# Cross-attention scored three tiles ahead, and a convolution in rounds of two blocks, in a twelve-sublayer kernel

## The chip, the cores and the metric

The kernel runs on one core of a Trainium2 chip. The metric is the device time of one execution in microseconds, as the median of several runs. The engines are PE (matrix products, with its weight loads PEld), DVE (vector), ACT (activation functions), POOL, and SP, which here only issues transfers.

## What is computed

A model of four layers with three sublayers each works on 2 x 1024 tokens of width 256 in float32. Each sublayer is added to its input and the sum normalised. The change touches two of the twelve:

```python
def _L2_xattn_ref(query, key, value, Wq, bq, Wk, bk, Wv, bv, Wo, bo):
    Q = jnp.einsum('bsd,de->bse', query, Wq) + bq
    K = jnp.einsum('bsd,de->bse', key, Wk) + bk
    V = jnp.einsum('bsd,de->bse', value, Wv) + bv
    scale = 1.0 / jnp.sqrt(jnp.asarray(D, Q.dtype))
    scores = jnp.einsum('bqd,bkd->bqk', Q, K) * scale
    attn = jax.nn.softmax(scores, axis=-1)
    out = jnp.einsum('bqk,bkd->bqd', attn, V)
    return jnp.einsum('bsd,de->bse', out, Wo) + bo
...
def _L3_attn_ref(x, W_in, conv_w, conv_b, W_out):
    h = jnp.einsum('bld,df->blf', x, W_in)
    a, g = jnp.split(h, 2, axis=-1)
    h = a * jax.nn.sigmoid(g)
    hc = jnp.transpose(h, (0, 2, 1))
    y = lax.conv_general_dilated(hc, conv_w, window_strides=(1,), padding=[(K - 1, 0)], ...) + conv_b[None, :, None]
    y = jax.nn.silu(y)
    y = jnp.transpose(y, (0, 2, 1))
    return jnp.einsum('blf,fd->bld', y, W_out)
```

The attention has one head of width 256 and 154 keys. The convolution is causal, with 4 taps, and each of its 512 channels has its own weights.

## The kernel before

Activations are held feature-major (`XT`, 128 partitions x 2 chunks x 2048 tokens) and token-major (`Xtok`, 16 tiles of 128 tokens). Each sublayer is a row of phases. A `phase` opens a block in which every engine runs its own list in the order of the code, with waits on counting semaphores; a barrier of all engines ends it. Nothing of a phase overlaps the next one. There are eight PSUM banks of 128 x 512 floats, `K.bank`. On an engine an instruction that reads what the one before it wrote has a `drain` or a semaphore wait ahead of it.

**Attention, `L2_xattn` (from L895).** After the projections one phase (L913) goes through `NT` = 16 tiles of 128 tokens. For each tile PE scores it (`score`, L924: 128 x 154), DVE takes the row maximum and scales it (`maximum`, L957 and L959), ACT takes the exponential with the row sum as a second result (L984), DVE takes the reciprocal of the sum and multiplies (L971, L973), PE transposes the result in two pieces (L945, L946), and ACT copies these into `PT` (L997, L998). For each block of four tiles PE multiplies with the values (`values`, L934), both halves of the features in a row, and DVE copies the result out (`output`, L964). PE scores tile t+1 ahead of the transposes of tile t. Scores have two banks (0, 1), as `probs` has two buffers, transposes two banks (2, 3) and value products four (4 to 7). After a block's fourth tile its values come behind the next tile's transposes.

**Convolution, `L3_attn` (from L1060).** One phase (L1074) goes through 16 blocks of 128 channels x 512 tokens. For each PE computes a and g (L1089; block n uses the pair of banks n % 4), ACT takes the sigmoid of g (L1100), DVE multiplies it by a into `H` (`gate`, L1120), and then computes the four taps into `acc`: a scaling with bias (L1132), and three multiply-adds in place (L1135), each behind a drain. ACT takes the sigmoid of the result (L1105) and POOL multiplies the two into `Y` (L1112). `sg`, `ss` and `acc` have two buffers each. DVE gates one block ahead, and ACT takes the second sigmoid two blocks behind the first. SP issues the load of the output weights `Wout` at the start of the phase.

Both sublayers end with `finish` (L139), which multiplies by the output weights, adds, normalises and turns back; the transfers of the next sublayer's weights are issued at its start.

## Time and profile before

| | us |
|---|---|
| median of 3 runs | 3495.94 (3495.18 to 3498.05) |
| the profiled execution, its own time | 3497.36 |
| its span, first to last instruction | 3495.6 |
| attention phase of `L2_xattn` | 63.1 |
| convolution phase of `L3_attn` | 81.8, to the start of the next |

Over the span PE is busy 2866.3 us (82%), DVE 1939.8 (55%), ACT 1564.7 (45%), POOL 712.8 (20%). These are averages over twelve different sublayers and say little on two phases that are 4% of the span together; those are read from their own stretches, below. All times in rows are microseconds from the span's start. The trace counts each float32 matmul as two instructions, the order below as one.

### The profile page before, as it was taken

How to read it: one execution, taken by the hardware profiler on the slowest of the kernel's cores; microseconds unless marked ns; L12 is line 12 of the kernel's file. 1: busy time of each engine (PE TensorE's matmuls, PEld its weight loads, DVE VectorE, ACT ScalarE, POOL GpSimd, SP SyncE). 2: the span in 40 equal slices, each digit the busy share in tenths (PEclk: the TensorE clock that was granted, in tenths of full speed). 3: DMA queues.
4: the chain of work that ended last, by engine and by line, in shares of the span. 5: the costliest groups of instructions: out<-in, count | busy, mean ns of one | idle time of the engine just before them, and what ended most of it. 6: DMA issues, size and time to landing. Idle time of an engine off the chain costs nothing. (4 is left out here: it accounts for less than half of the span.)

```text
span 3495.6 us, 54010 instructions
## 1 busy us (share of the span) xinstructions
PE 2866.3 (82%) x18533; PEld 1739.5 (50%) x18565; DVE 1939.8 (55%) x4670; ACT 1564.7 (45%) x4333; POOL 712.8 (20%) x790
## 2 busy tenths in 40 slices
PE   6586994845999998679968998989988968959993
PEld 3443562332555555345634653446533445639993
DVE  6546674343878876576726662156522647842333
ACT  4313782322777776572224562135521228813331
POOL 3201010021211220012104560045500102301113
PEclk9686996868999999889978999999999989959996
DMA  1000002010000000000001001000000000051112
GB/s 68 1 2 14 1 2 79 0 55 12 1 1 2 1 2 24 37 13 1 17 0 38 1 1 59 0 6 1 1 27 12 7 21 2 2 223 32 36 36 80
DMA packets 34789, 80.46 MB, mean 23 GB/s; under 512 B 8577, under 2 KB 23570, under 8 KB 30450
## 3 DMA queue, kind: packets, MB, share of 16 engines
q1 hardware_dynamic: 29746, 64.61, 5.1%
q0 software_dynamic: 4368, 11.93, 1.2%
q8 instruction: 137, 2.24, 0.3%
q14 instruction: 106, 0.87, 0.1%
q10 hardware_dynamic: 432, 0.80, 0.1%
HBM read 63.31 MB, written 14.02 MB: 22 GB/s over the span
## 5 line engine op out<-in xcount | busy, mean ns | idle before, releaser
L2436 ACT ACTIVATE scores<-scores,min 128x128 f32<-128x128 f32 (+7 forms) x256 | 198.5, 775 | 86.1 <-DVE min L2419 82.1
L2417 DVE TENSOR_SCALAR zero_marks<-psum 128x128 f32<-128x128 f32 (+7 forms) x256 | 192.0, 750 | 66.6 <-PE psum L2349 64.8
L2419 DVE CUSTOM_DVE_ANT_0 scores<-psum,zero_marks 128x128 f32<-128x128 f32 (+7 forms) x256 | 193.9, 758 | 29.9 <-issue 0.9
L2356 PE MATMUL psum<-ident,scores 128*128 128x128 f32 x1152 | 172.8, 277 | 16.4 <-ACT probsT L2453 13.3
L2453 ACT ACTIVATE probsT<-psum 128x128 f32<-128x128 f32 (+7 forms) x256 | 163.0, 637 | 31.7 <-PE psum L2356 31.1
L3684 PE MATMUL psum<-Hn,W 128*128 128x512 f32 x384 | 170.1, 606 | 8.2 <-PEq L415 8.2
L1574 ACT ACTIVATE XT<-psum,b_of_tile 128x128 f32<-128x128 f32 x312 | 89.0, 368 | 177.5 <-PE psum L1494 177.5
L1494 PE MATMUL psum<-x_gatheredT,XT 128*128 128x128 f32 x1248 | 152.0, 281 | 6.0 <-issue 3.1
L1494 PEld LDWEIGHTS psum<-x_gatheredT,XT 128*128 128x128 f32 x1248 | 147.1, 196 | 12.9 <-issue 11.8
L2356 PEld LDWEIGHTS psum<-ident,scores 128*128 128x128 f32 x1152 | 123.2, 141 | 55.8 <-issue 29.8
L2346 PE MATMUL psum<-XT,Q_heads 64*128 64x512 f32 x256 | 143.7, 641 | 0.0
L3542 POOL TENSOR_TENSOR probs<-probs,stat 128x512 f32<-128x512 f32 (+1 forms) x128 | 123.2, 986 | 99.8 <-DVE stat L3506 97.3
L1503 PE MATMUL psum<-W,XT 128*128 x624 | 141.2, 379 | 0.6 <-DVE y L1548 0.6
L3556 ACT ACTIVATE probs<-psum,stat 128x256 f32<-128x256 f32 (+1 forms) x256 | 114.4, 460 | 47.1 <-DVE stat L3499 47.1
L3410 POOL TENSOR_TENSOR straight<-straight,crossed 128x512 f32<-128x512 f32 x64 | 81.1, 1268 | 224.6 <-DVE crossed L3400 224.6
L3684 PEld LDWEIGHTS psum<-Hn,W 128*128 128x128 f32 x384 | 74.7, 195 | 103.7 <-issue 103.7
L1503 PEld LDWEIGHTS psum<-W,XT 128*128 128x128 f32 x624 | 115.5, 190 | 15.1 <-issue 1.0
L3700 DVE SCALAR_TENSOR_TENSOR GT<-psum,b,gelu 128x512 f32<-128x512 f32 x48 | 36.0, 751 | 142.0 <-ACT gelu L3694 142.0
L3499 DVE TENSOR_REDUCE stat<-psum 128x2 f32<-128x512 f32 (+1 forms) x128 | 78.1, 652 | 50.7 <-PE psum L3450 22.2
L848 ACT ACTIVATE probs<-probs,stat 128x154 f32<-128x154 f32 x256 | 104.9, 412 | 2.7 <-DVE stat L786 2.7
L2347 PE MATMUL psum<-XT,Q_heads_turned 64*128 64x128 f32 (+3 forms) x256 | 102.8, 482 | 0.0
L2340 PE MATMUL psum<-XT,Q_heads 128*128 128x128 f32 (+3 forms) x256 | 96.2, 458 | 3.3 <-POOL Q_heads L2318 2.8
(619 smaller groups left out, 6860.8 us busy)
## 6 DMA issues: line engine op xcount, KB each, us to landing
W<-in_L3f_W SPq DMA_DIRECT2D x16, 1024.0 KB, 22.5
L3f_y_rows<-y SPq DMA_DIRECT2D x39, 128.0 KB, 1.7
L0f_rows<-Xtok SPq DMA_DIRECT2D x2, 2048.0 KB, 7.7
W<-in_L0f_W SPq DMA_DIRECT2D x3, 1152.0 KB
early_weights<-in_L2f_Wqkv SPq DMA_DIRECT2D x2, 1536.0 KB
W<-in_L2f_W SPq DMA_DIRECT2D x2, 1536.0 KB
XT<-in_xT SPq DMA_DIRECT2D x1, 2048.0 KB, 10.3
Xtok<-in_xtok SPq DMA_DIRECT2D x1, 2048.0 KB
```

The lines of the kernel that those rows point to most:

```text
L848: last = act.activation(p, src, ACT.Exp, bias=st(n, 0)[:, h:h + 1], scale=-1.0, accum_out=st(n, 1)[:, h:h + 1])
L1494: ins = pe.matmul(K.bank[2 * q + part][:, m * P:(m + 1) * P], W1t[:, k * INTER + (part * HALF + m) * P:k * INTER + (part * HALF + m + 1) * P],
L1503: ins = pe.matmul(K.bank[6][:, 0:D], HT[:, q, c, :], W2[:, bass.ds(at + c * D, D)], start=(c == 0), stop=(c == IC - 1))
L2346: pe.matmul(sc(i)[:, 0:BLK], Qh[own, u % 2, h, :], KT[own, c, b * S:b * S + BLK], start=True, stop=True, skip_group_check=True)
L2356: ins = pe.transpose(turned[:, kt * P:(kt + 1) * P], Sc[:, i % ROT, kt * P:(kt + 1) * P], K.ident[:])
L2417: dve.tensor_scalar(zero[:, i % 2, 0:n], sc(i)[:, 0:n], 0.0, -NEG, ALU.is_equal, ALU.mult)
L2419: dve.tensor_tensor_reduce(Sc[:, i % ROT, 0:n], sc(i)[:, 0:n], zero[:, i % 2, 0:n], 1.0, -NEG, ALU.add, ALU.min, low[:, i % ROT:i % ROT + ...
L2436: act.activation(p, p, ACT.Exp, bias=low[:, i % ROT:i % ROT + 1], scale=-1.0, accum_out=sums[:, u % 2, h:h + 1]).then_inc(s["exp_done"], 1)
L2453: act.activation(PT[:, i % SLOTS, 0:n], turned[:, 0:n], ACT.Copy).then_inc(s["pt_out"], 1)
L3542: pool.tensor_tensor(v, v, inner(stat[:, t % 2, 2, 2 * g:2 * g + 2], ks.stop - ks.start), ALU.mult).then_inc(s["normed"], 1)
L3556: act.activation(Pr[:, t % 2, h, ks], K.bank[2 * G + hh][:, c0 + ks.start:c0 + ks.stop], ACT.Exp, bias=stat[:, t % 2, 0, h:h + 1], scale=- ...
L3684: ins = pe.matmul(K.bank[2 * (n % 4) + part][:], W1[:, k, (part * HC + m) * P:(part * HC + m + 1) * P], Hn[:, k, j * BLK:(j + 1) * BLK], s ...
```

## The change

In the attention phase scores get four banks (0, 1, 6, 7) and are computed three tiles ahead; value products keep banks 4 and 5, and their two halves are put behind the transposes of two successive tiles. `probs` has three buffers, and the statistics are three tiles of four columns each. On DVE the maximum of tile t+2 stands between the reciprocal and the normalising of tile t, with a semaphore in place of the drain. ACT takes the exponential of tile t+2 behind the copies of tile t, where it took that of t+1 ahead of them.

In the convolution two blocks make a round. ACT takes both sigmoids of round r, then silu of the two blocks of round r-2 straight into `Y`, as one function, then the first tap of both blocks of round r. DVE gates both blocks of round r and then runs taps 1 to 3 of round r-1, alternating between its blocks, with semaphores in place of drains. POOL keeps only the zeroing of the padding. `sg` has four buffers, `acc` six, and `ss` is gone.

PE in the attention phase before, from the scores of tile 4 on (`probs` are normalised scores; `V` are values, `KT` and `QT` keys and queries):

```order
L924 MATMUL psum<-KT,QT 128x154 x2
L945 MATMUL psum<-ident,probs 128x128
L946 MATMUL psum<-ident,probs 26x128
L934 MATMUL psum<-probsT,V 128x512 x4
L924 MATMUL psum<-KT,QT 128x154 x2
L945 MATMUL psum<-ident,probs 128x128
```

PE there in the change, at the start of the phase and from the scores of tile 7 on:

```order
L925 MATMUL psum<-KT,QT 128x154 x8
L945 MATMUL psum<-ident,probs 128x128
L946 MATMUL psum<-ident,probs 26x128
L925 MATMUL psum<-KT,QT 128x154 x2
...
L925 MATMUL psum<-KT,QT 128x154 x2
L945 MATMUL psum<-ident,probs 128x128
L946 MATMUL psum<-ident,probs 26x128
L934 MATMUL psum<-probsT,V 128x512 x2
L925 MATMUL psum<-KT,QT 128x154 x2
L945 MATMUL psum<-ident,probs 128x128
L946 MATMUL psum<-ident,probs 26x128
L934 MATMUL psum<-probsT,V 128x512 x2
```

Eight score matmuls instead of four come ahead of the first transposes, and the four value matmuls of a block are in two pairs, with a tile's scores and transposes between them.

ACT in the convolution before, from the start of the phase (`Y` is the result, `conv` the accumulator):

```order
L1100 ACT_TABLE_LOAD
L1100 ACTIVATE sigmoid<-psum 128x512 x3
L1105 ACTIVATE sigmoid_of_conv<-conv 128x512
L1100 ACTIVATE sigmoid<-psum 128x512
L1105 ACTIVATE sigmoid_of_conv<-conv 128x512
```

ACT there in the change, from the sigmoids of the third round to the sigmoid table's return:

```order
L1109 ACTIVATE sigmoid<-psum 128x512 x2
L1114 ACT_TABLE_LOAD
L1114 ACTIVATE Y<-conv 128x512 x2
L1122 ACTIVATE conv<-H,early_weights 128x512 x2
L1109 ACT_TABLE_LOAD
L1109 ACTIVATE sigmoid<-psum 128x512 x2
```

The sigmoid of the convolution's result, one a block, has turned into silu, the first taps (L1122) have come to ACT, and two loads of function tables stand in each round from here on; before there is one in the whole phase.

The diff, of the attention phase:

```diff
-        Pr = sbuf(es, nc, "probs", [P, 2, CTX])
+        Pr = sbuf(es, nc, "probs", [P, 3, CTX])
...
-        stat = sbuf(es, nc, "stat", [P, 2, 3])
...
+        low, total, recip = (sbuf(es, nc, n, [P, 4]) for n in ("low", "total", "recip"))
+        score_bank = lambda t: K.bank[(0, 1, 6, 7)[t % 4]]
...
                 def score(t):
-                    if t >= 2:
-                        pe.wait_ge(s["exp_done"], t - 1)
+                    if t >= 4:
+                        pe.wait_ge(s["exp_done"], t - 3)
                     for k in range(DC):
-                        last = pe.matmul(K.bank[t % 2][:, 0:CTX], QT[:, k, t * P:(t + 1) * P], KT[:, k, (t // 8) * 256:(t // 8) * 256 + CTX],
+                        last = pe.matmul(score_bank(t)[:, 0:CTX], QT[:, k, t * P:(t + 1) * P], KT[:, k, (t // 8) * 256:(t // 8) * 256 + CTX],
...
-                def values(j):
+                def values(j, h):
                     pe.wait_ge(s["probs_out"], TPB * (j + 1))
-                    if j >= 2:
-                        pe.wait_ge(s["out"], DC * (j - 1))
-                    for h in range(DC):
-                        for kt in range(2):
-                            last = pe.matmul(K.bank[4 + 2 * (j % 2) + h][:], V[:, j // 2, kt, h * P:(h + 1) * P], PT[:, j % 2, kt, :],
-                                             start=(kt == 0), stop=(kt == 1))
+                    if j >= 1:
+                        pe.wait_ge(s["out"], DC * (j - 1) + h + 1)
+                    for kt in range(2):
+                        last = pe.matmul(K.bank[4 + h][:], V[:, j // 2, kt, h * P:(h + 1) * P], PT[:, j % 2, kt, :], start=(kt == 0), stop=(kt == 1))
                     last.then_inc(s["pv_done"], 1)
 
-                score(0)
+                for t in range(3):
+                    score(t)
                 for t in range(NT):
-                    if t + 1 < NT:
-                        score(t + 1)
+                    if t + 3 < NT:
+                        score(t + 3)
                     pe.wait_ge(s["normed"], t + 1)
                     if t >= 2:
                         pe.wait_ge(s["probs_out"], t - 1)
-                    pe.transpose(K.bank[2 + t % 2][:, 0:P], Pr[:, t % 2, 0:P], K.ident[:])
-                    pe.transpose(K.bank[2 + t % 2][0:CTX - P, P:2 * P], Pr[:, t % 2, P:CTX], K.ident[:]).then_inc(s["turned"], 1)
-                    if t % TPB == 0 and t:
-                        values(t // TPB - 1)
-                values(NB - 1)
+                    pe.transpose(K.bank[2 + t % 2][:, 0:P], Pr[:, t % 3, 0:P], K.ident[:])
+                    pe.transpose(K.bank[2 + t % 2][0:CTX - P, P:2 * P], Pr[:, t % 3, P:CTX], K.ident[:]).then_inc(s["turned"], 1)
+                    if t % TPB in (0, 1) and t >= TPB:
+                        values(t // TPB - 1, t % TPB)
+                for h in range(DC):
+                    values(NB - 1, h)
 
...
-                maximum(0)
+                    dve.tensor_scalar(low[:, t % 4:t % 4 + 1], low[:, t % 4:t % 4 + 1], -scale, None, ALU.mult).then_inc(s["max_done"], 1)
...
+                def output(j, h):
+                    dve.wait_ge(s["pv_done"], DC * j + h + 1)
+                    dve.tensor_copy(OT[:, h, j * BLK:(j + 1) * BLK], K.bank[4 + h][:]).then_inc(s["out"], 1)
+
+                for t in range(2):
+                    maximum(t)
                 for t in range(NT):
-                    if t + 1 < NT:
-                        maximum(t + 1)
                     dve.wait_ge(s["exp_done"], t + 1)
-                    dve.reciprocal(stat[:, t % 2, 2:3], stat[:, t % 2, 1:2])
-                    dve.drain()
-                    dve.tensor_scalar(Pr[:, t % 2, :], Pr[:, t % 2, :], stat[:, t % 2, 2:3], None, ALU.mult).then_inc(s["normed"], 1)
-                    if t % TPB == 2 and t > TPB:
-                        output(t // TPB - 1)
-                output(NB - 1)
+                    dve.reciprocal(recip[:, t % 4:t % 4 + 1], total[:, t % 4:t % 4 + 1]).then_inc(s["recip_done"], 1)
+                    if t + 2 < NT:
+                        maximum(t + 2)
+                    dve.wait_ge(s["recip_done"], t + 1)
+                    dve.tensor_scalar(Pr[:, t % 3, :], Pr[:, t % 3, :], recip[:, t % 4:t % 4 + 1], None, ALU.mult).then_inc(s["normed"], 1)
+                    if t % TPB in (2, 3) and t > TPB:
+                        output(t // TPB - 1, t % TPB - 2)
+                for h in range(DC):
+                    output(NB - 1, h)
...
             @block.scalar
             def _(act):
                 def exp(t):
                     act.wait_ge(s["max_done"], t + 1)
-                    if t >= 2:
-                        act.wait_ge(s["turned"], t - 1)
-                    act.activation(Pr[:, t % 2, :], K.bank[t % 2][:, 0:CTX], ACT.Exp, bias=stat[:, t % 2, 0:1], scale=scale,
-                                   accum_out=stat[:, t % 2, 1:2]).then_inc(s["exp_done"], 1)
+                    if t >= 3:
+                        act.wait_ge(s["turned"], t - 2)
+                    if t >= 4:
+                        act.wait_ge(s["recip_done"], t - 3)
+                    act.activation(Pr[:, t % 3, :], score_bank(t)[:, 0:CTX], ACT.Exp, bias=low[:, t % 4:t % 4 + 1], scale=scale,
+                                   accum_out=total[:, t % 4:t % 4 + 1]).then_inc(s["exp_done"], 1)
 
                 act.wait_ge(s["zeroed"], 1)
                 exp(0)
+                exp(1)
                 for t in range(NT):
-                    if t + 1 < NT:
-                        exp(t + 1)
+                    j = t // TPB
                     act.wait_ge(s["turned"], t + 1)
...
-                        act.wait_ge(s["pv_done"], j - 1)
+                        act.wait_ge(s["pv_done"], DC * (j - 1))
...
+                    if t + 2 < NT:
+                        exp(t + 2)
```

and of the convolution:

```diff
-            sg, ss = (sbuf(inside, nc, n, [P, 2, BLK]) for n in ("sigmoid", "sigmoid_of_conv"))
-            acc = sbuf(inside, nc, "conv", [P, 2, BLK])
+            sg = sbuf(inside, nc, "sigmoid", [P, 4, BLK])
+            acc = sbuf(inside, nc, "conv", [P, 6, BLK])
...
+                ROUNDS = N // 2
...
-                @block.scalar
-                def _(act):
-                    for n in range(N + 2):
-                        if n < N:
-                            act.wait_ge(s["done"], n + 1)
-                            if n >= 2:
-                                act.wait_ge(s["h_done"], n - 1)
-                            act.activation(sg[:, n % 2, :], K.bank[2 * (n % 4) + 1][:], ACT.Sigmoid).then_inc(s["gated"], 1)
-                        if n >= 2:
-                            act.wait_ge(s["conv_done"], n - 1)
-                            if n >= 4:
-                                act.wait_ge(s["silu_done"], n - 3)
-                            act.activation(ss[:, n % 2, :], acc[:, n % 2, :], ACT.Sigmoid).then_inc(s["silu_gated"], 1)
-
                 @block.gpsimd
                 def _(pool):
                     pool.memset(H[:, :, :, 0:TAPS - 1], 0.0).then_inc(s["padded"], 1)
-                    for n, (m, j) in enumerate(steps):
-                        pool.wait_ge(s["silu_gated"], n + 1)
-                        pool.tensor_tensor(Y[:, m, j * BLK:(j + 1) * BLK], acc[:, n % 2, :], ss[:, n % 2, :], ALU.mult).then_inc(s["silu_done"], 1)
+
+                @block.scalar
+                def _(act):
+                    def gate_sigmoid(n):
+                        act.wait_ge(s["done"], n + 1)
+                        if n >= 4:
+                            act.wait_ge(s["h_done"], n - 3)
+                        act.activation(sg[:, n % 4, :], K.bank[2 * (n % 4) + 1][:], ACT.Sigmoid).then_inc(s["gated"], 1)
+
+                    def silu(n):
+                        m, j = steps[n]
+                        act.wait_ge(s["conv_done"], n + 1)
+                        act.activation(Y[:, m, j * BLK:(j + 1) * BLK], acc[:, n % 6, :], ACT.Silu).then_inc(s["silu_done"], 1)
+
+                    def tap0(n):
+                        m, j = steps[n]
+                        b, o = divmod(j * BLK, S)
+                        act.wait_ge(s["h_done"], n + 1)
+                        if n >= 6:
+                            act.wait_ge(s["silu_done"], n - 5)
+                        act.activation(acc[:, n % 6, :], H[:, m, b, o:o + BLK], ACT.Identity, scale=cw[:, m, 0:1], bias=cb[:, m:m + 1]).then_inc(s["tap0_done"], 1)
+
+                    act.wait_ge(s["padded"], 1)
+                    for r in range(ROUNDS + 2):
+                        for i in range(2):
+                            if r < ROUNDS:
+                                gate_sigmoid(2 * r + i)
+                        for i in range(2):
+                            if r >= 2:
+                                silu(2 * (r - 2) + i)
+                        for i in range(2):
+                            if r < ROUNDS:
+                                tap0(2 * r + i)
...
-                        dve.tensor_tensor(H[:, m, b, TAPS - 1 + o:TAPS - 1 + o + BLK], K.bank[2 * (n % 4)][:], sg[:, n % 2, :],
-                                          ALU.mult).then_inc(s["h_done"], 1)
+                        dve.tensor_tensor(H[:, m, b, TAPS - 1 + o:TAPS - 1 + o + BLK], K.bank[2 * (n % 4)][:], sg[:, n % 4, :], ALU.mult).then_inc(s["h_done"], 1)
+
+                    def tap(n, i, before, after):
+                        m, j = steps[n]
+                        b, o = divmod(j * BLK, S)
+                        dve.wait_ge(before, n + 1)
+                        dve.scalar_tensor_tensor(out=acc[:, n % 6, :], in0=H[:, m, b, o + i:o + i + BLK], scalar=cw[:, m, i:i + 1],
+                                                 in1=acc[:, n % 6, :], op0=ALU.mult, op1=ALU.add).then_inc(after, 1)
 
                     dve.wait_ge(s["padded"], 1)
-                    gate(0)
-                    for n, (m, j) in enumerate(steps):
-                        b, o = divmod(j * BLK, S)
-                        if n + 1 < N:
-                            gate(n + 1)
-                        dve.wait_ge(s["h_done"], n + 1)
-                        if n >= 2:
-                            dve.wait_ge(s["silu_done"], n - 1)
-                        dve.tensor_scalar(acc[:, n % 2, :], H[:, m, b, o:o + BLK], cw[:, m, 0:1], cb[:, m:m + 1], ALU.mult, ALU.add)
-                        for tap in range(1, TAPS):
-                            dve.drain()
-                            ins = dve.scalar_tensor_tensor(out=acc[:, n % 2, :], in0=H[:, m, b, o + tap:o + tap + BLK], scalar=cw[:, m, tap:tap + 1],
-                                                           in1=acc[:, n % 2, :], op0=ALU.mult, op1=ALU.add)
-                        ins.then_inc(s["conv_done"], 1)
+                    for r in range(ROUNDS + 1):
+                        for i in range(2):
+                            if r < ROUNDS:
+                                gate(2 * r + i)
+                        if r >= 1:
+                            dve.wait_ge(s["h_done"], 2 * r)
+                            for i, before, after in ((1, s["tap0_done"], s["tap1_done"]), (2, s["tap1_done"], s["tap2_done"]), (3, s["tap2_done"], s["conv_done"])):
+                                for n in (2 * r - 2, 2 * r - 1):
+                                    tap(n, i, before, after)
```

## Rows read from the trace of the kernel before

**Rows 1.** Windows: length, busy us (count) of PE, PEld, DVE, ACT, POOL, PEclk, DMA, GB/s
```profile
1779.50:1842.60 63.10, 41.81 (x128) 23.66 (x128) 18.41 (x72) 15.63 (x65) 0.95 (x1) 0.73 0.00 1
1785.00:1790.00 5.00, 2.82 (x11) 2.19 (x11) 1.68 (x8) 1.64 (x8) 0.00 (x0) 0.50 0.00 0
1795.00:1800.50 5.50, 5.50 (x9) 2.45 (x10) 0.00 (x0) 0.42 (x2) 0.00 (x0) 0.58 0.00 1
2746.00:2798.00 52.00, 51.80 (x121) 22.53 (x119) 45.82 (x57) 13.44 (x24) 14.37 (x10) 1.00 0.00 0
```

**Rows 2.** In order of time, one tile at full clock: start, length, engine, line, operation, count [idle before]
```profile
1802.73 0.33 PE L945 MATMUL psum<-ident,probs 128*128 128x128 f32 x1 [1.09 <-DVE probs L973]
...
1803.01 0.69 PE L924 MATMUL psum<-KT,QT 128*128 128x154 f32 x4
1803.21 0.28 ACT L997 ACTIVATE probsT<-psum 128x128 f32<-128x128 f32 x1 [0.47 <-PE psum L946]
...
1803.73 0.32 DVE L957 TENSOR_REDUCE stat<-psum 128x1 f32<-128x154 f32 x1 [1.06 <-PE psum L924]
...
1804.32 0.39 ACT L984 ACTIVATE probs<-psum,stat 128x154 f32<-128x154 f32 x1 [0.69 <-DVE stat L959]
1804.43 0.30 DVE L973 TENSOR_SCALAR probs<-probs,stat 128x154 f32<-128x154 f32 x1
...
1804.79 0.33 PE L945 MATMUL psum<-ident,probs 128*128 128x128 f32 x1 [1.09 <-DVE probs L973]
```

**Rows 3.** In order of time, further rows of the attention phase
```profile
1782.30 0.39 ACT L984 ACTIVATE probs<-psum,stat 128x154 f32<-128x154 f32 x1
...
1782.81 0.16 DVE L971 RECIPROCAL stat<-stat 128x1 f32<-128x1 f32 x1 [1.37 <-ACT probs L984]
...
1786.70 1.23 PE L924 MATMUL psum<-KT,QT 128*128 128x154 f32 x4
...
1809.21 3.60 PE L934 MATMUL psum<-probsT,V 128*128 128x512 f32 x8
...
1841.31 1.29 DVE L964 COPY OT<-psum 128x512 f32<-128x512 f32 x2 [7.80 <-PE psum L934]
```

**Rows 4.** The score line alone: duration in ns min/median/max
```profile
L924 PE MATMUL psum<-KT,QT x64: 294/294/467, 1779.6 to 1830.5; 128*128 128x154 f32 x64
```

**Rows 5.** In order of time, the convolution phase and the start of the next
```profile
2740.20 57.60 PE L1089 MATMUL psum<-XT,early_weights 128*128 128x512 f32 x128 [1.10 <-PEq L415]
...
2789.81 1.44 POOL L1112 TENSOR_TENSOR Y<-conv,sigmoid_of_conv 128x512 f32<-128x512 f32 x1 [2.94 <-ACT sigmoid_of_conv L1105]
...
2791.86 1.58 DVE L1135 SCALAR_TENSOR_TENSOR conv<-H,early_weights,conv 128x512 f32<-128x512 f32 x2
...
2793.36 0.68 DVE L1120 TENSOR_TENSOR H<-psum,sigmoid 128x512 f32<-128x512 f32 x1
...
2793.96 0.54 DVE L1132 TENSOR_SCALAR conv<-H,early_weights 128x512 f32<-128x512 f32 x1
...
2819.83 1.26 POOL L1112 TENSOR_TENSOR Y<-conv,sigmoid_of_conv 128x512 f32<-128x512 f32 x1 [2.11 <-ACT sigmoid_of_conv L1105]
...
2821.81 14.89 PE L162 MATMUL psum<-Wout,Y 128*128 128x256 f32 x56 [24.01 <-PEq L415]
```

**Rows 6.** DVE alone in a narrow stretch: the first multiply-add of a block
```profile
2790.20 1.59 DVE L1135 SCALAR_TENSOR_TENSOR conv<-H,early_weights,conv 128x512 f32<-128x512 f32 x1
```

**Rows 7.** ACT in other sublayers: silu, a PSUM copy, a table load, Identity with scale and bias
```profile
27.17 0.63 ACT L2896 ACTIVATE act_T<-conv 128x512 f32<-128x512 f32 x1 [0.21 <-DVE conv L2913]
27.71 0.58 ACT L2890 ACTIVATE raw<-psum 128x512 f32<-128x512 f32 x1
...
1995.38 1.28 ACT L3378 ACT_TABLE_LOAD   x1
1996.68 0.21 ACT L3378 ACTIVATE norm<-norm 128x8 f32<-128x8 f32 x1
...
2156.34 1.52 ACT L2186 ACTIVATE Hn<-Hn,ln_scale_bias 128x512 f32<-128x512 f32 x2 [6.04 <-DVE Hn L2168]
```

16 lines of the change are left out of this document (5 added, 11 removed).

## The prediction

> **What bounds the kernel now.** I read the busy time of each engine over both changed phases first, then one cycle of each phase in order of time, then single rows elsewhere for the prices of operations that are new here. The twelve sublayers run one behind the other on one core, each phase ending at a barrier, so every microsecond by which a phase ends earlier is one off the span.
>
> The attention phase of `L2_xattn` runs from PE's first score at 1779.6 to the last output copy, 1841.31 + 1.29 = 1842.6 [rows 3]. No engine fills it: PE is busy 41.8 of 63.1 us, DVE 18.4, ACT 15.6, at a mean clock of 0.73 [rows 1]. One tile at full clock shows the ring [rows 2]. From transpose to transpose it takes 1804.79 - 1802.73 = 2.06: 0.28 to the next score's start, 0.72 until DVE takes its maximum, 0.59 until ACT's exponential, 0.11 to DVE's normalising (of the tile before), 0.36 to PE again. PE is busy under half of that, and from 1785 to 1790, where it is so, the granted clock is 0.50, which is 1.2 GHz [rows 1]. The value products, eight matmuls, take 3.60 at full clock [rows 3], and while they run DVE and ACT have nothing to do.
>
> The convolution of `L3_attn` runs from 2740.20 to POOL's last product, 2819.83 + 1.26 = 2821.09; PE's first matmul of the next phase is at 2821.81 [rows 5]. PE's 128 matmuls form one group of 57.60 us that ends at 2797.8 [rows 5], so PE hardly waits. The last 23.3 us are a backlog of DVE. A block on DVE is a gate with a pitch of 0.60 (2793.36 to 2793.96), tap 0 (0.54, and 0.07 for the drain), a first multiply-add of 1.59 [rows 6] and two of 1.58 together [rows 5], with 0.08 for the drain between these and 0.08 of overlap with the next gate: 4.38 a block. PE needs 8 x 0.43 = 3.43 (57.60 less a slower start, over 16). A multiply-add alone is 0.75 ((1.58 - 0.08) / 2); the one of 1.59 is the one that lies beside POOL's product of 1.44 [rows 5].
>
> **Attention, part by part.** No work goes or comes: 64 score matmuls in the trace's counting, 32 transposes and 32 value matmuls stay, and so do DVE's and ACT's instructions. What changes is who waits. The score tiles in four banks, the third buffer for probabilities and the four statistics are free, as they only hold results longer.
> PE per tile at full clock: transposes 0.28, scores (0.69 - 0.29) / 3 x 4 = 0.53 [rows 2, 4], together 0.80. Values of a block 3.44, as two halves of 1.72 (the group's 3.60 less the last one's tail). At half clock a score group is 1.23 [rows 3], so (1.23 - 0.47) / 3 x 4 = 1.0 a tile [rows 4], and transposes 0.5: 1.5.
> The new ring goes over two tiles, since the exponential of tile t+2 stands behind the copies of tile t. From transpose t to transpose t+2: copies start after 0.48 [rows 2], the exponential some 0.33 later (two copies of 0.28 and less, overlapping), the reciprocal 0.51 behind it (1782.81 after 1782.30 [rows 3]) with a pitch of 0.08, then the maximum of tile t+2 and its scaling, which now stand between reciprocal and normalising, 0.47 (0.59 less the 0.12 of the hand-over to ACT), normalising to PE 0.36. Sum 2.23, or 1.1 a tile: tiles without values are bound by this ring (1.1 against 0.80), those with values by PE.
> Four tiles in steady state: PE's work is 4 x 0.80 + 3.44 = 6.64. Only the two tiles behind the second half of the values lie closer than 2.23 apart (2 x 0.80), which adds 0.6, and DVE's output copies, now one in front of each of two reciprocals, add about 0.25. That gives 7.5.
> In sequence: the first transposes come at 1782.81 + 0.08 + 0.47 + 0.36 = 1783.7, later than before by the extra maximum. Four tiles at half clock reach 1789.7, two blocks of 7.5 reach tile 12 at 1804.7. Tiles 12 to 15 have both halves of block 2's values but one less wait: 3 x 0.27 + 3.44 = 4.25, so 1808.9. Then 1.0 until the last turned probabilities are out, values 3.6, last copy 0.7: **1814.2** instead of 1842.6. Gain **28.4 us**.
> The clock is the doubtful term. PE has no gap worth naming from 1783.7 on. Where it worked unbroken before, from 1795.0 to 1800.5, the stretch has 0.58, so it rose towards its end; in the convolution, busy 51.8 of 52.0, it stays at 1.00 [rows 1]. I let it rise near 1789. Bounds: never half, 2 us less; risen only behind the values of block 0, 4.4 more (3.44 for the values and 0.8 for a tile); never risen is rival 1.
>
> **Convolution, part by part.** POOL's 16 products leave, and with them the stretch of the multiply-add beside them, 1.59 - 0.75 = 0.84 a block. Tap 0 leaves DVE, 0.61 a block. The drains leave, since the taps of two blocks alternate and each waits only for the tap before last: the pitch of a multiply-add falls from 0.83 with a drain to 0.75 - 0.08 = 0.67, the 0.08 being the overlap that the gate at 2793.36 has with the multiply-adds that end at 2791.86 + 1.58 [rows 5]. The other bound is that each such wait costs what a drain does, 0.83. I take 0.67, since that gate waits on a semaphore too. DVE per round of two blocks: 2 x 0.60 + 6 x 0.67 = 5.2 (6.2 at the bound) against PE's 2 x 3.43 = 6.86. DVE no longer decides.
> ACT now has, per round, two sigmoids, two silus, two first taps and **two table loads**, which stand in the order of the change in every round from the third: twelve loads more. An activation of 512 columns out of PSUM is 0.58, a silu 0.63 with 0.54 to the next one's start; a first tap is an Identity with scale and bias from memory, 1.52 for two of 128x512 [rows 7]. A load is 1.28, shows no idle time ahead, and the next activation starts at 1996.68, 1.30 behind 1995.38 [rows 7]. Round: 0.49 + 0.58 + 2 x 1.30 + 2 x 0.54 + 1.52 = 6.27, below 6.86 by only 0.59. The first sigmoid of a round starts some 2.4 us late behind the load, which costs nothing: PE needs its bank pair back three blocks later. The load itself waits for a gate that is long done, not for PE.
> So PE goes on as before and ends at 2797.8. Behind it: sigmoid and gate, 1.4; six taps of blocks 12 and 13, 4.0, for which nothing is left to cover; six of 14 and 15, 4.1; silu 0.6: 10.1. End 2807.9 instead of 2821.1, gain **13.2 us**. With 0.83 a tap it is 12 x 0.16 = 1.9 less. The output weights are issued at the phase's start as before, 60 us ahead of use. The next phase starts from an idle PE in both, so I leave its length.
> A rule speaks against this part. The Trainium skill, ScalarE: Activation LUTs, section What ACT_TABLE_LOAD costs, puts a switch to another set at about 2.66 us, of which 1.38 are a drain, and says to batch calls by set. The trace agrees with its 1.28 but shows no drain beside the load of [rows 7]. By the page's figure, as an estimate, a round would be 9.0 and the sum about 12 us higher, near rival 2.
>
> **Sum.** 3495.6 - 28.4 - 13.2 = 3454.0 of span, and 1.76 around it (3497.36 - 3495.6) gives 3455.8 for a profiled execution. That one lay 1.42 above the median of the runs, so the median comes to 3495.94 - 41.6 = **3454.3**.
>
> **Rivals.**
> 1. *The clock stays at half through the attention phase.* For: it was 0.50 over most of the first 15 us. Against: PE was then busy half the time, and now nearly always. PE alone takes 12 x 1.0 (scores after the first four) + 16 x 0.5 + 4 x 6.9 = 47.6 from 1783.7; with 1.8 of tail the phase ends near 1833. Gain 9.5 + 13.2: **3473**.
> 2. *A table switch drains ACT for as long again as it loads*, 2.6 each. A round takes 6.27 + 2.6 = 8.9, PE waits for the gates, the five rounds between full ones lose 2.0 each and the tail 0.5: **3465**. For: the margin is small. Against: the activation that starts 0.02 behind a load.
> 3. *Slower: ACT becomes the convolution's bound altogether.* One mechanism, the switches between sigmoid's and silu's tables from 2755 to 2798: each us of extra x in a switch costs 5 x (2x - 0.59) + x. The whole gain of 41.6 us is used up at x = 4.0, a switch of 5.3 us; at 6.0 us a switch the time is **3503**. Nothing in the profile speaks for it.
> 4. *The attention ring does not open*, PE still waits for DVE at each tile. The order of the change has four tiles' scores ahead of the first transposes and three ahead of each later pair, so this can only be a longer hand-over here or there; 0.3 us at each of 16 tiles is 5, inside the range.
>
> **How the numbers follow.** Forecast 0.76, its own range 3450 to 3460 (clock 2 less or 4.4 more, taps 1.9 more). Rival 1 0.10, rival 2 0.08, rival 3 0.02, gain eaten to within 0.2% 0.02, better than 3450 0.02. The range that holds 8 in 10 reaches from 3449 to 3467, to rival 2. About 0.2%, 7 us, is what a measurement of this kernel can tell from no change: faster 0.96, same 0.02, slower 0.02.
>
> **What would show it.** Attention phase: some 35 us long, granted clock above 0.85, PE busy over 85%, DVE's and ACT's instructions as long as now. Convolution: multiply-adds at 0.75 throughout, PE's group still 57.6 long, twelve more loads with activations 0.02 behind them, 10 us from PE's last matmul to the end. The forecast is wrong if PE waits for gates in the convolution (ACT bound), or if score matmuls still read 0.47 in the second half of the attention phase (clock).

## The result and the profile after

The changed kernel takes **3449.66 us** (median of 4 runs, 3449.26 to 3451.57), the one before 3495.56 beside it (3490.76 to 3498.05). The ratio is 0.9874, 95% interval 0.9860 to 0.9887, or 45.9 us less. Forecast were 41.6 less, 3454.3; the time lies 0.7 above the lower end of the range of 3449 to 3467. The profiled execution took 3451.57, its span is 3449.8.

The stretches of the two phases, and the first tiles of the attention phase (length, busy us and count of PE, PEld, DVE, ACT, POOL, PEclk, DMA share, GB/s), answer to [rows 1]:

```profile
1774.70:1807.40 32.70, 27.68 (x128) 17.47 (x128) 17.33 (x72) 13.86 (x65) 0.94 (x1) 1.00 0.00 1
2704.70:2773.20 68.50, 57.57 (x128) 25.14 (x129) 42.75 (x64) 45.91 (x61) 0.05 (x1) 0.92 0.02 8
1774.70:1779.00 4.30, 2.49 (x17) 2.28 (x18) 1.87 (x10) 2.13 (x5) 0.94 (x1) 1.00 0.00 0
1779.00:1783.20 4.20, 3.26 (x24) 2.73 (x22) 2.62 (x15) 3.06 (x16) 0.00 (x0) 1.00 0.02 4
```

The attention phase is 32.7 us long instead of 63.0, with DVE and ACT about as busy as before (17.3 and 13.9 us, against 18.4 and 15.6) and PE busy 85% of it at a granted clock of 1.00. The convolution phase is 68.5 instead of 81.6; POOL has left it, DVE has 42.75 us of work, ACT 45.91, PE the same 57.6.

In order of time, PE's transposes at four places of the attention phase, and DVE's last copy (start, length, engine, line, operation, count, and what ended the idle time before it):

```profile
1778.84 0.33 PE L945 MATMUL psum<-ident,probs 128*128 128x128 f32 x1 [1.78 <-DVE probs L974]
...
1783.22 0.33 PE L945 MATMUL psum<-ident,probs 128*128 128x128 f32 x1 [0.48 <-DVE probs L974]
...
1790.53 0.33 PE L945 MATMUL psum<-ident,probs 128*128 128x128 f32 x1 [0.36 <-DVE probs L974]
...
1797.85 0.33 PE L945 MATMUL psum<-ident,probs 128*128 128x128 f32 x1 [0.36 <-DVE probs L974]
...
1806.73 0.69 DVE L964 COPY OT<-psum 128x512 f32<-128x512 f32 x1 [1.03 <-PE psum L934]
```

These are tiles 0, 4, 8 and 12: 4.38 us for four tiles without values, then 7.31 and 7.32 for four with them. From the waits of the same stretch, what PE still waits for (us in total, times, longest):

```profile
PE psum L945 <- DVE probs L974: 3.5, 5, 1.8
```

The longest, 1.78 us at the first tile, holds a load of ACT's table for the exponential:

```profile
1776.16 1.28 ACT L988 ACT_TABLE_LOAD   x1 [9.51 <-DVE low L960]
```

ACT stood idle for 9.51 us before it. No run here moves this load ahead of the phase.

One round of the convolution on ACT and its end, in order of time; these answer to [rows 5 to 7]:

```profile
2755.44 0.60 ACT L1109 ACTIVATE sigmoid<-psum 128x512 f32<-128x512 f32 x1 [0.49 <-PE psum L1095]
2756.05 1.28 ACT L1114 ACT_TABLE_LOAD   x1
2757.35 1.15 ACT L1114 ACTIVATE Y<-conv 128x512 f32<-128x512 f32 x2
2758.40 1.51 ACT L1122 ACTIVATE conv<-H,early_weights 128x512 f32<-128x512 f32 x2
2759.93 1.28 ACT L1109 ACT_TABLE_LOAD   x1
2761.22 0.60 ACT L1109 ACTIVATE sigmoid<-psum 128x512 f32<-128x512 f32 x1
2762.30 0.60 ACT L1109 ACTIVATE sigmoid<-psum 128x512 f32<-128x512 f32 x1 [0.48 <-PE psum L1095]
...
2763.54 8.03 DVE L1148 SCALAR_TENSOR_TENSOR conv<-H,early_weights,conv 128x512 f32<-128x512 f32 x12
...
2770.94 1.29 ACT L1114 ACTIVATE Y<-conv 128x512 f32<-128x512 f32 x2 [2.68 <-DVE conv L1148]
```

A round is 2762.30 - 2755.44 = 6.86, PE's pace. The second sigmoid still waits 0.49 for PE: ACT keeps up. All 48 multiply-adds, by their source line (duration in ns, min/median/max), are of one length:

```profile
L1148 DVE SCALAR_TENSOR_TENSOR conv<-H,early_weights,conv x48: 740/744/748, 2722.3 to 2770.8; 128x512 f32<-128x512 f32 x48
```

**Where the 45.8 us of span went** (3495.6 - 3449.8), by the starts of the phases: 4.9 ahead of the attention phase, where nothing was changed (1779.6 to 1774.7); 30.3 in it; 0.3 between the two; 13.1 in the convolution (next phase at 2773.20 instead of 2821.81); and 2.8 lost behind it. So the two phases give **43.4 us**, and the other 2.4 (4.9 and 0.3 less the 2.8) come from places that the change left alone.

### The profile page after: what moved, and what is told of

It is laid out like the page before. It is cut to its first block and busy times, and to the rows that moved or that the text cites. A ratio compares the mean times of both kernels' runs of the same rounds, so it can differ in the third digit from the quotient of the medians.

```text
span 3449.8 us, 53931 instructions
## 1 busy us (share of the span) xinstructions
PE 2849.0 (83%) x18533; PEld 1729.9 (50%) x18565; DVE 1914.0 (55%) x4654; ACT 1588.8 (46%) x4360; POOL 690.0 (20%) x774
## 5 line engine op out<-in xcount | busy, mean ns | idle before, releaser
L2379 PEld LDWEIGHTS psum<-ident,scores 128*128 128x128 f32 x1152 | 123.2, 141 | 55.9 <-issue 30.3
```

Of the source, the lines that this page charges most:

```text
L2379: ins = pe.transpose(turned[:, kt * P:(kt + 1) * P], Sc[:, i % ROT, kt * P:(kt + 1) * P], K.ident[:])
```

## Experiments

Each kernel was timed beside the kernel before on the same chip. Lengths of phases are read as above: attention from PE's first score to the end of DVE's last copy, convolution from PE's first matmul to PE's first of the next phase.

### The kernel before once more

No edit.

> The kernel before once more, unchanged, for the parts of the program that the change does not touch. Theory (the change made only its two phases shorter; the 4.8 us by which the trace of after is ahead at 870 us, and the 3 us that it gives back behind 3113 us, differ from one execution to the next): this trace shifts by 1 to 5 us against the first one of the kernel before in the same places (near 540, 590 and behind 3145 us), and nowhere else. Rival (the change itself, by other addresses or code, moves the sublayers ahead of 870 us): this trace is within 0.5 us of the first one everywhere up to 1752 us.

Measured: 3493.23 (3490.61 to 3496.59, 10 runs) against 3494.26 (16 runs), ratio 0.9995 [0.9986, 1.0005]. Its attention phase is 63.1 long, its convolution 81.7. One line that lies ahead of both phases, in the profile of before and of before again (first and last start); in that of after it starts at 682.9 too:

```profile
L2708 PE MATMUL psum<-ident,gates x4: 369/417/417, 687.0 to 687.6; 128*9 128x128 f32 x4
```
```profile
L2708 PE MATMUL psum<-ident,gates x4: 369/417/417, 682.9 to 683.5; 128*9 128x128 f32 x4
```

The same kernel reaches this point 4.1 us earlier in one execution than in another. Its attention phase starts at 1775.2, against 1779.6 in the first execution and 1774.7 in the changed kernel: 4.4 of the 4.9 us ahead of the phase belong to the execution that I had worked from, not to the change. Over all profiled kernels of this study the point above lies anywhere from 680.8 to 687.0. The 2.8 us lost behind lie in one group of matmuls, in the profiles of before and of after:

```profile
L1494 PE MATMUL psum<-x_gatheredT,XT x1248: 272/275/575, 3145.4 to 3430.1; 128*128 128x128 f32 x179
```
```profile
L1517 PE MATMUL psum<-x_gatheredT,XT x1248: 272/275/574, 3096.7 to 3384.3; 128*128 128x128 f32 x179
```

It is 284.7 long in before and 287.6 in after. Here the theory of this run, which expected a shift behind 3145 as well, did not come true: before_again has 284.7 too. With the new convolution the group is 286.0 to 287.7 long in six kernels of the study and 283.5 and 283.6 in the other two (four_loads and pool_back below); in the six kernels without it, it is 282.1 to 285.8. So the kernels with the new convolution lean to the longer side, each in a single profiled execution, and whether the change has a part in it stays open.

### Each part alone

The change to `L2_xattn` without that to `L3_attn`, and the other way round.

> The attention phase of the change, the convolution of before. Theory: the attention phase shrinks by 30.2 us, as in the trace of after, with the clock at 1.00 throughout, and the convolution keeps its 81.6 us; total 30 less than before, so about 3465. Rival (the two parts help or hurt each other): a phase length that differs from after's by over 1 us.

> The convolution of the change, the attention phase of before. Theory: the convolution ends 13.1 us earlier after its start than before, with PE's group still 57.6 us; attention keeps its 63.1 us at a clock near 0.73; total 13 less than before, about 3482. Rival: as for the other half, a phase length that differs from after's by over 1 us.

Measured: attention alone 3463.00, ratio 0.9911 [0.9894, 0.9927], attention phase 32.8, convolution 81.7. Convolution alone 3483.74, ratio 0.9973 [0.9961, 0.9984], phases 63.1 and 68.6. The windows of the attention phase in the first and of the convolution in the second:

```profile
1776.70:1809.50 32.80, 27.68 (x128) 17.47 (x128) 17.38 (x72) 13.87 (x65) 0.95 (x1) 1.00 0.00 1
```
```profile
2733.00:2801.64 68.64, 57.66 (x129) 25.21 (x129) 42.76 (x64) 45.92 (x61) 0.12 (x1) 0.92 0.02 8
```

In their phases the parts gain 30.3 and 13.0 and do not touch each other. In the whole time they gain 31.3 and 10.5, which add to 41.8; the difference to 43.4 is inside the intervals.

### Attention: how far ahead, and the clock

Two tiles of scores ahead instead of three, otherwise the change:

```diff
-                for t in range(3):
+                for t in range(2):
...
-                    if t + 3 < NT:
-                        score(t + 3)
+                    if t + 2 < NT:
+                        score(t + 2)
```

> The change, with PE scoring tiles two ahead instead of three (all banks and buffers as in the change), so that the scores of tile t+2 stand directly ahead of the transposes of tile t, whose normalising stands on DVE behind the maximum of tile t+2. Theory (the gain is from the length of the lead, which takes PE's scores out of the ring): the ring is 0.28 to the scores, 0.72 to the maximum, 0.47 to the normalising, 0.36 to PE, 1.83 a tile, and the values, 3.44 a block, come on top: 10.8 us for four tiles instead of 7.3, so the phase is 12 to 14 us longer than after's at full clock, and more (up to 25) if PE's gaps then bring the clock down. Rival (the gain comes from the clock or from splitting the values, and two ahead would do): the phase is within 2 us of after's.

Measured: 3465.19, ratio 0.9920 [0.9903, 0.9936]; the attention phase is 47.5, 14.8 longer than with three. PE in order of time, and two windows:

```profile
1779.56 0.33 PE L945 MATMUL psum<-ident,probs 128*128 128x128 f32 x1 [2.31 <-DVE probs L974]
...
1781.37 0.33 PE L945 MATMUL psum<-ident,probs 128*128 128x128 f32 x1 [0.85 <-DVE probs L974]
...
1781.65 1.05 PE L925 MATMUL psum<-KT,QT 128*128 128x154 f32 x4
...
1784.03 1.23 PE L925 MATMUL psum<-KT,QT 128*128 128x154 f32 x4
```
```profile
1783.50:1789.00 5.50, 3.75 (x14) 2.80 (x15) 1.66 (x9) 1.57 (x8) 0.00 (x0) 0.50 0.01 3
1800.00:1823.00 23.00, 16.45 (x62) 8.59 (x60) 9.15 (x33) 6.00 (x31) 0.00 (x0) 1.00 0.00 0
```

With two ahead PE stands still 0.85 at every tile, a tile takes 1.81 at full clock, and at 1781.65 the four score matmuls begin to stretch, from 0.69 to 1.23. From there the stretch has 0.50. So the third tile ahead is worth twice: it closes PE's gap, and with the gap goes the loss of clock. The gap is the larger part. From the transposes of tile 1 to those of tile 5 are 12.50 us (1781.37 to 1793.87); at full clock, later in the same phase, a tile takes 1.81 and one with half of the values 3.53, which would make 3 x 1.81 + 3.53 = 8.96. So about 3.5 of the 14.8 us are the clock's, as an estimate, and 11.3 the gap's. From 1800 on the same waits of 0.85, with values among them, leave the clock at 1.00.

The other way to part ring and clock is to leave the order of before and fill PE's gap with work whose results nobody reads, three more matmuls a tile ahead of each transpose (this kernel adds work; the ring is that of before):

```diff
                         score(t + 1)
-                    pe.wait_ge(s["normed"], t + 1)
                     if t >= 2:
                         pe.wait_ge(s["probs_out"], t - 1)
+                    for k in range(3):
+                        pe.matmul(K.bank[2 + t % 2][:, 2 * P:2 * P + CTX], QT[:, 0, t * P:(t + 1) * P], KT[:, 0, 0:CTX], start=True, stop=True)
+                    pe.wait_ge(s["normed"], t + 1)
```

> The kernel before, with three more score matmuls (six in the trace's counting) per tile behind the scores in the attention phase, into a part of a bank that nobody reads, so that PE works in the gap in which it waited for DVE. The order, the banks and the ring of the kernel before stay. Theory (of the 30.3 us that the change gained there, part is the ring and part is that PE's clock no longer falls): the six fit into the gap (0.28 + 0.53 + 0.8 = 1.6 of the ring's 2.06), the granted clock is 1.00 throughout, twelve tiles take 2.06 and three with values 5.5, and with a start of 3.9 and an end of 5.7 the phase is 50 to 52 us instead of 63, though PE has more to do. Then the clock is about 12 of the 30.3 and the ring 18. Rival (the ring is all of it, the clock only follows): the phase stays at 63 or grows by what PE has more to do.

Measured: 3480.89, ratio 0.9953 [0.9938, 0.9967]. Its window over the phase, and two transposes in a row:

```profile
1775.80:1827.30 51.50, 43.72 (x224) 31.52 (x224) 18.37 (x72) 15.68 (x65) 0.87 (x1) 0.97 0.00 1
```
```profile
1794.23 0.33 PE L947 MATMUL psum<-ident,probs 128*128 128x128 f32 x1 [0.31 <-DVE probs L975]
...
1795.04 0.95 PE L945 MATMUL psum<-KT,QT 128*128 128x154 f32 x6
...
1796.29 0.33 PE L947 MATMUL psum<-ident,probs 128*128 128x128 f32 x1 [0.30 <-DVE probs L975]
```

PE does 224 matmuls instead of 128 and the phase is 11.5 us **shorter**, since the granted clock is 0.97 instead of 0.73; the ring takes 2.06 a tile, as in [rows 2]. So of the 30.3 us of the change some 11.5 are the clock's, and 18.8 the ring's. This is the division when the clock is mended first; two_ahead, where the lead comes first, leaves another.

How the phase begins, in the kernel before (two windows) and in this one:

```profile
1779.50:1781.00 1.50, 1.28 (x8) 1.08 (x8) 0.55 (x3) 0.00 (x0) 0.95 (x1) 1.00 0.00 0
1783.00:1785.00 2.00, 1.59 (x6) 1.27 (x6) 0.30 (x1) 0.57 (x4) 0.00 (x0) 0.50 0.00 0
```
```profile
1775.80:1777.50 1.70, 1.70 (x7) 1.70 (x8) 0.32 (x1) 0.00 (x0) 0.87 (x1) 0.50 0.00 0
```

The kernel before begins at 1.00 and has 0.50 once PE has waited 2.56 us for its first transposes. filled_gaps begins at 0.50 and is at 1.00 from 1779.5 on; the expectation was 1.00 throughout. PE's idle time ahead of the phase is the same in both, 2.28 us. Of the 14 profiled executions of this study only this one begins so, and nothing here tells why.

### Convolution: what made the backlog

The kernel before, with ACT's second sigmoid written straight to `Y` and POOL's product gone. This leaves out the factor `conv` in silu:

```diff
-                            act.activation(ss[:, n % 2, :], acc[:, n % 2, :], ACT.Sigmoid).then_inc(s["silu_gated"], 1)
+                            act.activation(Y[:, m, j * BLK:(j + 1) * BLK], acc[:, n % 2, :], ACT.Sigmoid).then_inc(s["silu_done"], 1)
...
-                        pool.tensor_tensor(Y[:, m, j * BLK:(j + 1) * BLK], acc[:, n % 2, :], ss[:, n % 2, :], ALU.mult).then_inc(s["silu_done"], 1)
```

> The kernel before, with POOL's product left out of the convolution: ACT writes the second sigmoid straight into the result, so the factor conv is missing. Everything else of the convolution is as before: tap 0 and three drains on DVE, block by block. Theory (the backlog of DVE was made by POOL, whose product of 1.44 stretches the multiply-add beside it from 0.75 to 1.59): all multiply-adds are 0.75, a block on DVE is 4.38 - 0.84 = 3.54, close to PE's 3.43, and the phase ends about 13 us earlier than before; that is as much as the whole change brings there. Rival (tap 0 and the drains made it, and POOL's product only lay at the end): only its last 1.3 to 2 us are gained.

Measured: 3482.41, ratio 0.9955 [0.9941, 0.9969], convolution **68.1**. Its window, and its multiply-adds by source line:

```profile
2736.30:2804.38 68.08, 57.47 (x128) 25.14 (x129) 53.13 (x80) 20.89 (x34) 0.04 (x1) 0.93 0.03 8
```
```profile
L1131 DVE SCALAR_TENSOR_TENSOR conv<-H,early_weights,conv x48: 750/751/753, 2747.6 to 2802.0; 128x512 f32<-128x512 f32 x48
```

With the drains and with tap 0 on DVE, this phase is as short as that of the whole change. DVE's 53.1 us fit under PE's 57.5. One could still think that DVE had waited for POOL to give back a buffer, and not that POOL stretched its work. The waits of DVE in the convolution of the kernel before (us in total, times, longest) speak against it; apart from 0.4 us they are these, for ACT:

```profile
DVE H L1120 <- ACT sigmoid L1100: 11.4, 2, 8.8
```

So the backlog came from the stretch beside POOL's product, 0.84 a block. Now the same with the right function, one silu behind each sigmoid in every block, so two table loads a block:

```diff
-                            act.activation(ss[:, n % 2, :], acc[:, n % 2, :], ACT.Sigmoid).then_inc(s["silu_gated"], 1)
+                            act.activation(Y[:, m, j * BLK:(j + 1) * BLK], acc[:, n % 2, :], ACT.Silu).then_inc(s["silu_done"], 1)
```

> The kernel before, with only this changed in the convolution: ACT takes silu of each block straight into the result, two blocks behind the sigmoid as before, and POOL has no product. Tap 0 and the drains stay on DVE, and there are no rounds. Theory (with POOL's product gone, DVE's 3.54 a block is enough, and what the rounds are for is to halve the table switches): ACT switches twice a block, 0.60 + 1.30 + 0.63 + 1.30 = 3.85 a block against PE's 3.43, so some 13 blocks lose 0.4 each and the phase, to PE's next matmul, is 71 to 73 us against 68.5 after and 81.6 before. Rival (the rounds and the first tap on ACT bring nothing at all): it is 68 to 69.

Measured: 3482.23, ratio 0.9956 [0.9940, 0.9973], convolution 71.9. ACT in order of time:

```profile
2761.23 0.60 ACT L1100 ACTIVATE sigmoid<-psum 128x512 f32<-128x512 f32 x1
2761.84 1.28 ACT L1104 ACT_TABLE_LOAD   x1
...
2763.78 1.28 ACT L1100 ACT_TABLE_LOAD   x1
2765.08 0.60 ACT L1100 ACTIVATE sigmoid<-psum 128x512 f32<-128x512 f32 x1
```

ACT takes 3.85 a block where PE takes 3.43, so ACT is the bound; PE's matmuls still end after 57.5 us, and the loss is ACT's backlog behind them. The simple edit brings 9.7 of the 13.1 us; rounds of two blocks, six buffers, tap 0 on ACT and no drains together bring the other 3.4. That this is by having two loads for two blocks fits the rows, but no run has these parts one by one.

### Convolution: the stretched multiply-add

The change, with a POOL product in each block that reads only constants and writes a tile of its own:

```diff
+                    for n in range(N):
+                        pool.wait_ge(s["tap0_done"], n + 1)
+                        if n:
+                            pool.wait_ge(s["pooled"], n)
+                        pool.tensor_tensor(dump[:], K.ones[:, 0:BLK], K.ones[:, 0:BLK], ALU.mult).then_inc(s["pooled"], 1)
```

> The change, with one product of 128x512 a block put on POOL again, on constants into a tile that nobody reads, released by the first tap of each block. Theory (POOL's work stretches a multiply-add that it runs beside): in each round two multiply-adds take about 1.6 instead of 0.75, DVE's round grows from 5.2 to 6.9, just PE's 6.86, so the phase is 1 to 4 us longer, all of it in the tail or the last rounds. Rival (the stretch came from POOL reading the same tiles as DVE, conv and the second sigmoid): multiply-adds stay at 0.75 and the phase keeps after's length within 0.5.

Measured (a single execution): 3453.16, convolution 69.8, 1.3 longer than in the change. DVE's and POOL's rows in order of time:

```profile
2760.01 1.04 POOL L1107 TENSOR_TENSOR dump<-ones 128x512 f32<-128x512 f32 x1 [4.38 <-ACT conv L1128]
2760.05 1.54 DVE L1154 SCALAR_TENSOR_TENSOR conv<-H,early_weights,conv 128x512 f32<-128x512 f32 x1
...
2761.19 1.30 POOL L1107 TENSOR_TENSOR dump<-ones 128x512 f32<-128x512 f32 x1
2761.52 1.52 DVE L1154 SCALAR_TENSOR_TENSOR conv<-H,early_weights,conv 128x512 f32<-128x512 f32 x1
```

No tile is shared, and still a multiply-add lasts 1.54 instead of 0.74. It ends 0.54 behind the product's end (2761.59 and 2761.05), the next one 0.55 (2763.04 and 2762.49). In the kernel before the same two ends are 0.54 apart (2790.20 + 1.59 [rows 6] and 2789.81 + 1.44 [rows 5]). In the other rounds of both kernels the first multiply-add that starts beside a product ends 0.54 to 0.56 behind it too. By these rows a multiply-add that starts while a product runs stands still until that is over. The Trainium skill, SBUF — State Buffer, section SBUF: two separate sides, says this: a VectorE operation with two SBUF inputs and a GpSimd operation that reads SBUF take a shared pair of ports as an exclusive lock, and whoever comes second is blocked until the first is done. All three ends agree with it. Here DVE is not the bound, so it costs only 1.3.

### Convolution: the table loads

Two tiny activations (128x1) ahead of the silus in the full rounds, which put two more loads in each; and all loads but the first away, with sigmoid in place of silu (this leaves out the factor `conv`):

```diff
+                        if 2 <= r < ROUNDS:
+                            act.activation(spare[:, r:r + 1], K.eps[:], ACT.Silu)
+                            act.activation(spare[:, 8 + r:9 + r], K.eps[:], ACT.Sigmoid)
```
```diff
-                        act.activation(Y[:, m, j * BLK:(j + 1) * BLK], acc[:, n % 6, :], ACT.Silu).then_inc(s["silu_done"], 1)
+                        act.activation(Y[:, m, j * BLK:(j + 1) * BLK], acc[:, n % 6, :], ACT.Sigmoid).then_inc(s["silu_done"], 1)
```

> The change, with two table switches more in each of the rounds 3 to 8 of the convolution, each made by an activation of one column (silu, then sigmoid, into a spare tile) ahead of the silus. Theory (ACT has 0.59 us to spare in a round, and a switch costs 1.30 and no drain): each round with them costs ACT 2 x 1.30 + 0.4 = 3.0 more and is 2.4 over PE's 6.86; five such rounds are 12, and the first taps of the last round come 2 late, so the phase is 12 to 15 us longer than after's, and PE now waits for gates. Rival (a switch costs as much again in a drain, hidden so far): over 20 us longer.

> The change, with sigmoid in place of silu in the convolution, so that no table is switched there and the result lacks the factor conv. Theory (PE bounds the rounds, and the loads lie in ACT's slack): twelve loads and 15.6 us of ACT go, PE's group stays 57.6, and the phase is shorter by the one load at most that stands in the tail, 0 to 0.2 us, since DVE's taps set the tail. Rival (the loads delay gates and so PE or DVE): over 1 us shorter.

Measured: four loads 3465.99, ratio 0.9917 [0.9900, 0.9934], convolution 82.3; no loads (a single execution) 3455.70, convolution 68.6. ACT with four loads, in order of time:

```profile
2744.61 1.08 ACT L1110 ACTIVATE sigmoid<-psum 128x512 f32<-128x512 f32 x2
2745.71 1.28 ACT L1131 ACT_TABLE_LOAD   x1
2747.01 0.20 ACT L1131 ACTIVATE spare<-eps 128x1 f32<-128x1 f32 x1
2747.22 1.28 ACT L1132 ACT_TABLE_LOAD   x1
2748.51 0.20 ACT L1132 ACTIVATE spare<-eps 128x1 f32<-128x1 f32 x1
2748.72 1.28 ACT L1115 ACT_TABLE_LOAD   x1
2750.01 1.15 ACT L1115 ACTIVATE Y<-conv 128x512 f32<-128x512 f32 x2
...
2753.88 1.08 ACT L1110 ACTIVATE sigmoid<-psum 128x512 f32<-128x512 f32 x2
```

A round takes 9.27. The three switches in a row take 1.30, 1.29 and 1.29 to the next activation, with no drain. The loads of the change cost nothing (68.5 with twelve in the phase, 68.6 with one), the next twelve 13.8 us; six rounds at 9.27 - 6.86 would be 14.5, and where the other 0.7 stays was not followed. Rival 3's formula, 5 x (2x - 0.59) + x, gives 13.6 for the 3.0 us that a round has more here (x = 1.5): it was right on what a longer switch would cost, but the switches are not longer. The way was not the one that this expectation and rival 2 give. PE waited for a gate once, 1.3 us, and its matmuls ended 59.2 us into the phase instead of 57.6; nearly all of the loss is ACT's backlog behind them.

### Two further steps

The exponential of tile t+2 ahead of the copies of tile t; and, on top, in the convolution's last full round, first taps ahead of the silus and the gates among the multiply-adds of the round before:

```diff
+                    if t + 2 < NT:
+                        exp(t + 2)
                     act.wait_ge(s["turned"], t + 1)
...
+                        if r == ROUNDS - 1:
+                            for i in range(2):
+                                tap0(2 * r + i)
...
+                            tap(n, 2, s["tap1_done"], s["tap2_done"])
+                            gate(2 * r)
+                            tap(n + 1, 2, s["tap1_done"], s["tap2_done"])
+                            gate(2 * r + 1)
```

> The change, with ACT's exponential of tile t+2 ahead of the copies of tile t instead of behind them. Theory (in the attention phase PE waits for normalised probabilities in five places, 3.5 us together, of which 1.78 is the first one, because the exponential stands behind copies that wait for PE): the ring over two tiles opens, the four later waits go and the phase is 0.8 to 1.7 us shorter. Rival (the copies, now behind the exponential, hold back the values, which need all four tiles turned): as long as after, or up to 0.5 longer.

> As exp_first, and in the last full round of the convolution the order is turned: DVE runs the taps of blocks 12 and 13 around the gates of 14 and 15 instead of behind them, and ACT takes the first taps of 14 and 15 ahead of the silus of 10 and 11. Theory (the 10 us between PE's last matmul and the end are two rows of six multiply-adds, of which one need not wait for PE): the convolution phase is 2.3 to 3 us shorter than after's 68.5, and nothing else changes; total 3 to 4.5 below after. Rival (the tail is bound by ACT, which still has four silus and a load to do): under 1 us shorter.

Measured: exp_first 3456.49, ratio 0.9884 [0.9868, 0.9901], attention 32.0, 0.7 less than the change and just short of the 0.8 expected. Two of PE's four later waits went, those of 0.48; two of 0.36 stayed, and so did the first (1.79), which holds the table load and not the copies that the expectation named. both_tails 3458.03 (3450.16 to 3459.06), ratio 0.9881 [0.9865, 0.9898], attention 32.0, convolution 66.9, 1.6 less; the expectation was 2.3 to 3. DVE at the end of the convolution in both_tails:

```profile
2769.90 0.68 DVE L1145 TENSOR_TENSOR H<-psum,sigmoid 128x512 f32<-128x512 f32 x1
```

The gate of block 14 comes at 2769.90 behind the multiply-adds, though its sigmoid ended at 2769.09: the order in which I wrote the taps may have given back part of what it won, 0.8 us at most. By their phases these two steps are 2.3 us faster than the change; in the whole time that can't be seen, and the 3 to 4.5 us expected did not show, as the executions differ by more in the sublayers that nobody touched. Whether both_tails is the faster kernel stays open.

## Why the prediction was right, point by point

- **The phase is the unit.** Right within what can be seen: the phases give 43.4 us, the median of the runs 45.9, and attention and convolution add up.
- **Attention ring.** Forecast 34.6, measured 32.7. The ring over two tiles, forecast 2.23, takes 2.20 and 2.18 (1778.84, 1781.04, 1783.22). The first transposes came 4.1 us behind PE's first score, as forecast; a block of four tiles with values took 7.3 where the sum had 7.5; tiles 12 to 15 took 1802.00 - 1797.85 = 4.15 where it had 4.25; the end 5.4 where it had 5.3.
- **The mis-sized term: the clock of the first four tiles.** The sum had "Four tiles at half clock", 6.0 us, and the clock rising near 1789. They took 4.38, all at 1.00. I had taken the 0.50 from 1785 to 1790 [rows 1] as what the first tiles get, but in the kernel before the phase starts at 1.00 too and falls behind a wait of PE, and with the gaps of the old ring filled it stays at 1.00 once it is there (filled_gaps). The prediction also calls PE busy under half of that stretch; the row has 2.82 of 5.00. The bound "never half, 2 us less" was the one that came true, and 1.6 of the 1.9 us are this. Rival 1 (half throughout) is then far off, as is rival 4: PE waits for DVE five times, 3.5 us in all, 1.8 of them at the first tile. "PE busy over 85%" was missed by a hair (27.68 of 32.70, 84.6%), by these waits.
- **Convolution.** Forecast 13.2, measured 13.1. A multiply-add pitches at (8.03 - 0.75) / 11 = 0.66, forecast 0.67. From the last sigmoid's start, 2762.30, to the end of the last silu, 2770.94 + 1.29 = 2772.23, are 9.9, forecast 10.1.
- **But the reasons were not equally needed.** The prediction listed POOL's product, tap 0 and the drains as three savings on DVE. no_product shows that the first alone lifts DVE's backlog. What tap 0 and the drains bring stands in no run by itself; together with the rounds, which halve the switches that a true silu needs, they bring 3.4 us (silu_each_block). The sum was right all the same, because it counted no saving on DVE beyond the point where PE bounds the phase.
- **Table loads.** 1.28 with 0.02 behind, as in [rows 7]; eleven more in the phase (12 against 1), where the prediction counted twelve. The figure of 2.66 a switch that the Trainium skill gives (ScalarE: Activation LUTs, What ACT_TABLE_LOAD costs) would have put the sum 12 us higher; no switch in the convolution phases of after, silu_each_block and four_loads took over 1.30 where the next activation had its input ready. The advice of the same page (section Table sets: the hidden batching unit) to batch calls by set held in four_loads and silu_each_block, where ACT is the bound, and bought nothing in no_loads, where it isn't.
- **The base.** Of what the span gained outside the phases, 4.4 us are the first profiled execution's, and the 2.8 lost behind stay open: before_again has 3491.4 of span for the same kernel. Against that one the change gains 3491.4 - 3449.8 = 41.6, less than the 43.4 of its phases; against the first, 45.8, more. Of the 4.6 us by which the forecast was too high, 1.8 lie in the phases (30.3 + 13.1 - 41.6), the rest in sublayers that nothing touched. The forecast's own range of 3450 to 3460 had no room for these: it held only the bounds of the changed phases, and the time lies 0.3 below it, in the case "better than 3450" that had a chance of 0.02. The range of 3449 to 3467 held by 0.7 us. The phases were forecast well; that the whole time fell inside the range is in part luck, since exp_first, with a phase 0.7 shorter, took 3456.49, 6.8 more (the kernel before, timed beside it, 3498.12).

## What to carry to other kernels

Before rebuilding a phase that DVE bounds, look whether its two-input operations are longer where POOL works on SBUF beside them; taking POOL away was here worth more than any reordering. Where an engine waits in a ring, count how many tiles of lead close the gap altogether: two gave 15.5 us, three 30.3, and about 3.5 of the difference were the clock's, which had fallen while PE waited. Table switches are free only in slack, so count the round against the pace of the engine that bounds it (6.27 forecast, and 6.86 - 0.49 = 6.37 measured, against 6.86 was enough; 9.27 was not). Look what the first wait of a phase holds; here it was a table load of 1.28 us behind 9.51 of idle time. And when costing a change, profile the kernel before twice, since an execution differs from the next by some microseconds in places that the change leaves alone.
